# A selective scan whose start is folded into its first input: ScalarE adds the old state, times the first decay, and all scans begin from zero

## What is computed

```python
def step(h, inp):
    dt_t, u_t, B_t, C_t = inp
    h = h * jnp.exp(dt_t[:, :, None] * A) + (dt_t * u_t)[:, :, None] * B_t[:, None, :]
    y = jnp.einsum('bdn,bn->bd', h, C_t)
    return (h, y)
h0 = jnp.zeros((Bb, D_INNER, D_STATE), x.dtype)
_, ys = jax.lax.scan(step, h0, xs)
```

## Time and profile before

| | us |
|---|---|
| median of 3 runs | 2238.55 (2237.41 to 2240.18) |
| profiled execution | 2238.26 |
| its span | 2236.5 |
| VectorE busy | 2047.3 (92%) |
| TensorE busy | 1847.3 (83%) |
| GpSimd busy | 1811.6 (81%) |
| ScalarE busy | 1342.3 (60%) |

### The profile page before, as it was taken

How to read it: one execution, slowest core, us unless ns; L and a number is a source line. 1 busy time by engine, 2 the same in 40 slices (tenths; PEclk the granted TensorE clock), 3 DMA queues, 4 the chain that set the end, 5 groups by cost and what they waited for, 6 DMA issues and landing times.

```text
span 2236.5 us, 24275 instructions
## 1 busy us (share of the span) xinstructions
PE 1847.3 (83%) x6152; PEld 765.3 (34%) x6153; DVE 2047.3 (92%) x2381; ACT 1342.3 (60%) x2404; POOL 1811.6 (81%) x652
## 2 busy tenths in 40 slices
PE   7687887878797879788787878797956699999997
PEld 3222332323232323233232323231312366655554
DVE  7899999999999999999999999999999877557776
ACT  3566757585766757675758576666755343424443
POOL 3389999999999999999999999999999434325444
PEclk9777988989898979798898989797967799999999
DMA  7734434343434344353534353444434462235554
GB/s 285 227 89 106 121 102 123 96 112 106 113 106 112 107 115 115 100 121 101 125 94 115 103 120 105 105 109 119 96 89 134 161 237 102 83 86 83 79 80 67
DMA packets 136494, 259.95 MB, mean 116 GB/s; under 512 B 19984, under 2 KB 42768, under 8 KB 135232
## 3 DMA queue, kind: packets, MB, share of 16 engines
q1 hardware_dynamic: 120064, 230.78, 38.8%
q0 software_dynamic: 13440, 17.93, 4.8%
q10 hardware_dynamic: 2880, 9.96, 1.1%
HBM read 190.32 MB, written 69.34 MB: 116 GB/s over the span
## 4 chain that ended last, share of the span: by engine, by line
DVE 47%; PE 22%; issue 14%; POOL 5%; ACT 4%; DMA 3%; DVEq 3%; SPq 1%; POOLq 0%; ACTq 0%
DVE hst L1364 30%; DVE dbu L1350 9%; PE psum L1764 4%; PE psum L1889 4%; POOL hst L810 3%; PE psum L1708 3%; PE psum L1722 2%; PE psum L1901 2%; PE psum L1752 2%; DVEq L1598 1%; DVE h L1608 1%; PE psum L1689 1%; DVE h L1620 1%; DMA b_rep<-bc_scratch 1%; ACT psum L1102 1%
## 5 line engine op out<-in xcount | busy, mean ns | idle before, releaser
L810 POOL TENSOR_TENSOR hst<-hst,c_rep 128x2048 f32<-128x2048 f32 x255 | 1152.1, 4536 | 22.6 <-ACT state L1090 20.1
L1102 ACT ACTIVATE psum<-dt_rep,neg_a 128x512 f32<-128x512 f32 x1024 | 692.8, 684 | 442.8 <-DVE hst L1364 433.8
L1364 DVE TENSOR_TENSOR_SCAN hst<-psum,state,dbu 128x512 f32<-128x512 f32 x768 | 919.3, 1257 | 0.0
L1350 DVE TENSOR_TENSOR dbu<-psum,b_rep 128x2048 f32<-128x2048 f32 x192 | 434.8, 2265 | 17.3 <-PE psum L1752 12.8
L1752 PE MATMUL psum<-dt,same 32*128 32x512 f32 x384 | 253.0, 743 | 192.8 <-DVE dbu L1350 184.5
L1764 PE MATMUL psum<-hst,same 128*32 128x512 f32 x2048 | 311.4, 763 | 50.3 <-POOL hst L810 42.0
L798 POOL TENSOR_TENSOR dbu<-dtu_rep,b_rep 128x2048 f32<-128x2048 f32 x64 | 291.7, 4558 | 45.8 <-DVE hst L1364 45.8
L1364 DVE TENSOR_TENSOR_SCAN hst<-psum,dbu 128x512 f32<-128x512 f32 x256 | 291.1, 1198 | 0.7 <-ACT psum L1102 0.7
L1708 PE MATMUL psum<-xp,taps 128*128 128x512 f32 x512 | 246.6, 632 | 5.6 <-ACTq L1019 4.8
L930 POOL DMA_INDIRECT out_x<-h,target_u x72 | 113.2, 1572 | 156.9 <-DMA out_x<-h,target_u 77.5
L1752 PEld LDWEIGHTS psum<-dt,same 32*128 32x128 f32 x384 | 64.9, 208 | 339.6 <-DVE dbu L1350 255.7
(11 more groups left out here) (175 smaller groups left out, 2236.8 us busy)
## 6 DMA issues: line engine op xcount, KB each, us to landing
dt_rep<-dt_scratch SPq DMA_DIRECT2D x256, 256.0 KB, 4.7
taps<-taps_scratch SPq DMA_DIRECT2D x64, 256.0 KB, 2.9
b_rep<-bc_scratch SPq DMA_DIRECT2D x64, 256.0 KB, 5.0
c_rep<-bc_scratch SPq DMA_DIRECT2D x64, 256.0 KB, 8.0
dt_scratch<-dt SPq DMA_DIRECT2D x64, 256.0 KB, 2.0
dtu_rep<-dtu_scratch SPq DMA_DIRECT2D x256, 64.0 KB, 1.9
h<-slot_scratch SPq DMA_DIRECT2D x72, 129.5 KB, 2.1
sp_tmp<-t_scratch SPq DMA_DIRECT2D x16, 512.0 KB, 4.9
```

The lines of the kernel that those rows point to most:

```text
L810: nc.gpsimd.tensor_tensor(h, h, c_rep[q % 2][:], ALU.mult).then_inc(prod_done, 1)
L1102: nc.scalar.activation(psum[:, PS_A + i, :], dt_rep[:, G % 2, j, :], ACT.Exp, scale=neg_a[:, q % 2, u, i:i + 1]).then_inc(exp_done, 1)
L1350: nc.vector.tensor_tensor(dbu[:, U % DBU, :, :], psum[:, PS_U:PS_U + 1, :].broadcast_to((P, NG, TB)), b_rep[U // UNITS % 2][:], ALU.mult). ...
L1364: nc.vector.tensor_tensor_scan(time_order(hst[:, U % RING, i, :], backward), time_order(psum[:, PS_A + i, :], backward), time_order(dbu[:, ...
```

## The change

`takes_state(U)` says whether a unit begins from a state (steps 2 to 7 and 10 to 15). In those, after the exponential of a group, ScalarE runs one more ACTIVATE on one column: dbu[first] = decay[first] * state + dbu[first], in place, where `first` is the first time step in the direction of time. It waits for the unit's multiply (at i == 0), for the state's copy and for the exponential, and counts up `seeded`. The scan waits for `seeded` in place of `exp_done`, and always begins from 0.0. `seed(T, n - 1)` is issued behind `decay(T, n)`, ahead of the other work of (T, n); `seed(T, 3)` behind all of the unit's iteration.

```diff
+def takes_state(U):
+    return U // UNITS // 2 % SEG > 0
+def seeds(U, i):
+    return NG * sum(takes_state(u) for u in range(U)) + i + 1
...
+            def seed(U, i):
+                q, u = divmod(U, UNITS)
+                first = 0 if q % 2 == 0 else TB - 1
+                if i == 0:
+                    mult_ready(act, U)
+                    act.wait_ge(state_saved, states_kept(U - 2 * UNITS))
+                act.wait_ge(exp_done, NG * U + i + 1)
+                at = dbu[:, U % DBU, i, first:first + 1]
+                nc.scalar.activation(at, psum[:, PS_A + i, first:first + 1], ACT.Identity,
+                                     scale=state[:, q % 2, u, i, :], bias=at).then_inc(seeded, 1)
...
                     decay(T, n)
+                    if takes_state(T) and n > 0:
+                        seed(T, n - 1)
...
                     if q + 2 < STEPS and (t, n) in XP_AT[:2]:
                         copy_xp(q + 2, XP_AT.index((t, n)))
+                if takes_state(T):
+                    seed(T, NG - 1)
...
-                start = 0.0 if q // 2 % SEG == 0 else state[:, q % 2, u, i, :]
-                dve.wait_ge(exp_done, NG * U + i + 1)
+                if takes_state(U):
+                    dve.wait_ge(seeded, seeds(U, i))
+                else:
+                    dve.wait_ge(exp_done, NG * U + i + 1)
                 nc.vector.tensor_tensor_scan(
...
-                    time_order(dbu[:, U % DBU, i, :], backward), start, ALU.mult, ALU.add).then_inc(scan_done, 1)
+                    time_order(dbu[:, U % DBU, i, :], backward), 0.0, ALU.mult, ALU.add).then_inc(scan_done, 1)
```

More of the change, by code:

```diff
@@ L377, in mixer_and_experts @@
         exp_done = sem("exp_done")
+        seeded = sem("seeded")
         scan_done = sem("scan_done")
```

## The result

The changed kernel takes 2261.09 us (median of 4 runs, 2259.64 to 2263.84), the kernel before, on the same chip, 2239.36. The ratio is 1.0101 (95% interval 1.0089 to 1.0114): 21.7 us slower. The profiled execution took 2259.87 us for a span of 2258.2. One execution further down, of the kernel whose seeds nobody waits for, took 2346.61 us at a granted TensorE clock of 0.77, where all others of this case had 0.86 to 0.88, and the ratio given there leaves it out.

The account below looks back on a forecast made before the run. VectorE, busy 624.11 of 624.73 us in the first stretch, bounds the kernel. Waits of 7.05 us against 3.84 gained give 35.3 us over 11 steps, step 15 gives -2.6: net +32.7, 2271 us, range 2240 to 2295.

Parts of the forecast that it names:

- The gain: VectorE's scans in 12 steps: starting from a constant saves 0.060 us each, 3.84 us a step, 46 us in all.
- The bound for seeds that cost nothing: All 12 changed steps: at most 12 x 1.8 = 22 us to be had, unless TensorE catches up.
- The seed: One-column ACTIVATE on ScalarE, 768 in all: 0.385 us long, taking 0.29 us of ScalarE's time.
- The rival of free operands: Small operands cost nothing, a seed is 0.20 us and takes 0.10: +10 us, 2248; chance 0.13.
- Unit 6: Last seed behind silu_xc and its two table loads, or late convolution copies: VectorE waits 3.3 us a step.
- Unit 8: Last seed behind copy_z and silu_z with its two table loads: VectorE waits 1.2 us a step.
- Unit 11: Last seed behind three softplus pieces and the logarithm: VectorE waits 1.65 us a step.
- Unit 2: seed(2, 1) behind copy_conv(2, 1), which waits for TensorE, and decay(2, 2): VectorE waits 0.9 us a step.
- Table loads: Units 6 and 8: 4.52 us for unit 6's load pair with silu; drain rule would give about 2335 us.
- The cover in unit 7: VectorE's stand for TensorE's spread_input, up to 2.15 us a step, lies behind the wait one unit earlier and is covered.
- What I cost at nothing: Seeds of units with no extra work, covered by ScalarE's wait for VectorE; without that cover 0.29 us each.
- VectorE keeps its pace: Rival: seeds come in time, steps run like steps 8 and 9: -22 us, 2216.5; chance 0.07.

Follow-up runs that it names:

- the half that removes: The kernel before with every scan started from the constant 0.0 and no seeds, the state left out: 2215.36 us against 2238.09.
- the half that adds, without its wait: The kernel before plus 768 one-column ACTIVATEs on SBUF alone into a spare column, result unused, VectorE not waiting for them: 2242.89 us against 2238.09.

## Why the prediction was right, and where its sizes were off

I had 2271 us, the run gave 2261.1: +21.7 us where I had +32.7. The mechanism was the one foretold, waits for seeds in four places of a step; a step of the first changed stretch takes 106.5 us in the mean (107.3 foretold), the steps 8 and 9 102 (102.3), step 15 96.8 (97). The term that was too large is the waits. Point by point:

- *The gain*: 0.060 us a scan, 46 us. Confirmed by the duration (1199 for 1257 ns) and by the account of the span. The bound for seeds that cost nothing, -22 us, is what the half that removes gave (-22.7).
- *The seed*: I took 0.385 us and 0.29 of ScalarE's time; it has 0.339 and 0.235 (1292.30 to 1292.53 in the fence above). Against the 200 ns of a small copy that is 139 more, less than the 193 ns that I had taken for the two operands from wide tiles; the seed also reads PSUM, so the 139 aren't the operands' alone. The rival of free operands, 0.20 and 0.10, falls. The Trainium skill (ScalarE: Activation LUTs, What ACT_TABLE_LOAD costs) has 373 ns as an estimate from its figures, 34 more than measured.
- *Unit 6*: 3.3 us foretold, 3.02 measured. *Unit 8*: 1.2 and 0.99. *Unit 11*: 1.65 and 1.22. *Unit 2*: 0.9 and 0.80. Together 7.05 and 6.0 a step; the difference of 1.0 us over 11 steps is the whole error of the forecast. In unit 6 the later of the two chains that I had worked out decides: in step 11 copy_conv(5, 1) starts at 1286.81, after 2.58 us of waiting for TensorE, and seed(6, 3) ends 11.67 us later (11.9 foretold). In unit 2 the mean agrees partly by luck: I had 0.45 to 1.35 us for the single wait, and they run from 0.19 to 1.80. In unit 11, where three seeds and the last one's end are on the chain, the smaller seed explains 0.2 us of 0.4; the rest I haven't traced.
- *Table loads*: 4.52 us for the pair with its silu, no drain beside the loads, as the rows before had it. With the drain of about 1380 ns for each switch that the Trainium skill (ScalarE: Activation LUTs, What ACT_TABLE_LOAD costs) adds, the wait in unit 6 would be near 6 us, as an estimate; the trace doesn't agree, it has 3.0.
- *The cover in unit 7*: I wrote that the stand for spread_input lies behind the wait in unit 6 and costs nothing. It did: it is missing from all changed steps of the trace after. That this cover also gave ScalarE time for unit 8, I had not seen.
- *What I cost at nothing*, the seeds of units without extra work: the half that adds, without its wait, shows 4.8 us for ScalarE's load without any wait on it, by way of save_state and GpSimd. In the changed kernel, with its longer steps, GpSimd waits 27.1 us for save_state instead of 38.1, and VectorE's waits ahead of its multiply haven't grown (11.9 us, 12.8 before). So by the trace nothing of this kind is in the 21.7.
- *The rivals*: "VectorE keeps its pace" named its condition, seed(6, 3) ready 3.27 us after the scan before, and said that only another order of the work could do it. The run with the last seed moved did exactly that and came to 2218, close to its 2216.5.

## What to carry to other kernels

Work taken from the engine that is the bound was given here to one with 40% idle time, and whether it paid hung on where it stood in the receiver's order: the same 768 instructions cost 22 us behind the long pieces that nobody had waited for and brought 19 ahead of them. Before moving such work, look for the time from the event that lets it start to the moment when it is wanted, at the worst place of the period, not for the sum. And directly behind the instruction whose result it reads wasn't the best place either: with one independent instruction between, ScalarE's period was 0.13 us shorter, and without it at the softplus pieces 22 us were lost, where GpSimd, a third engine, is busy 96 to 97% of a step. A wait that goes can also uncover another: only 19 of the 25 us of the units 8 and 11 arrived in the scans.

## What the runs showed of the hardware

- A scan with its start in a column of SBUF takes 59 ns more than one with a constant start, over 512 elements (1257 and 1198); in the kernel without the state all 1024 take 1198.
- A one-column ACTIVATE that reads PSUM, with scale and bias from SBUF, takes 339 ns and occupies the engine for 0.235 us when the next one doesn't depend on it.
- Seeds directly behind their exponentials in the units 9 to 12 cost 22 to 23 us. In the traces GpSimd's waits for save_state (a copy of 4 columns, 0.2 us) go from 23.9 to 46.8 us, ScalarE's for TensorE's sum from 22.2 to 46.0, and VectorE's in unit 2 of the next step from 8.6 to 31.0; that each leads to the next follows from the order of the work, and no run takes them apart.
